# Feed-forward block on one core: the spill of the token features split by halves, and a token tile's feature chain begun one step earlier

## Chip, core and metric

The kernel runs on one core of a Trainium2 chip. The metric is the device time of one execution in microseconds (us). The timed runs gave a median of 756.93 us (756.38 to 761.38, 3 runs).

## What is computed

The reference is one transformer block on 4 x 1024 tokens of 512 channels (cut to what matters):

```
x = x + layernorm(attn(layernorm(x)))                 # attention over channels
h = layernorm(x)
gate, up = h @ gate_w.T, h @ up_w.T                   # 512 -> 2048
x = x + layernorm((silu(gate) * up) @ down_w.T)       # 2048 -> 512
```

The three feed-forward weights are not given as matrices: each is a cubic interpolation (Catmull-Rom) of a short list of control points. The change lies in the second half of the program, the feed-forward block.

## The kernel before

The first half (up to about 389 us) does the attention and prepares the interpolation. The feed-forward half works on 8 groups of 512 tokens. Because the weights are smooth, a token's normalised row is first reduced to *features* (moments of pieces of the row), and gate and up are products of these features with unit coefficients (`s_all`), which stay in SBUF.

**Groups, quads, steps.** A group has 16 steps, one for each 128 of the 2048 hidden units; four steps are a *quad* (`quad`, with j for the quad and s for the step in it), and a quad handles one token tile of 128 tokens of a later group as well. In step i the engines do, each in its own written order:

- TensorE (PE): the gate and up matmuls of two steps ahead into `gbank` and `ubank` (line 1542), every second step a moment matmul into `mbank` (line 1558), and a quarter of an output tile of the group before (`part`: lines 1572 to 1574 and 1583 to 1585, into `ybank`). In step 1 of a quad it transposes a token tile (`feats.turn`, line 1073, into `turned`), in step 2 it multiplies it with the feature table (`feats.products`, lines 1083 to 1088, into `zbank` and `turned`).
- ScalarE (ACT): SiLU of gate (line 1373, `gated`), the upper half of the product in 16 bits (line 1369), the scaling of an output tile (`o_norm`, line 1391), and for the features `h_hi` (line 1021, step 0) and `z_hi` (line 1031, step 3, twice).
- VectorE (DVE): the product of gate and up (line 1442, `inter`), the statistics of an output tile (`o_stats`, line 1462, step 1), its last step (`o_finish`, line 1473, `x_res`, step 2), and for the features the statistics (`feats.stats`, line 1039, step 1), the normalisation (`feats.norm`, line 1046, `xn`, step 3), `h_lo` (line 1051, step 0), the copy of the transposed tile out of PSUM (`turn_copy`, line 1056, `hT`, step 2) and `z_lo` (line 1062, step 3).
- GpSimd (POOL): the lower half of the product, a subtraction (line 1328), and in step 1 three small operations for an output tile (`o_scale`, lines 1335 to 1339) and two for the features (`feats.scale`, lines 1013 and 1015).

All engines wait on each other by semaphores that count. `gbank`, `ubank`, `zbank` and `turned` are single banks: the next matmul into one waits until the last reader is done. The gate matmul of step i+2 waits for SiLU of step i+1, the up matmul for the product of step i+1.

**From features to `z`.** The features of a group's four tiles are collected in `z_hi` and `z_lo`. When the fourth is done, in quad 1 of the group before, SP writes them to DRAM (`feats.spill`) and reads them back in another arrangement as `z`, the moving operand of gate and up (`ffn_in.load_z`). Each goes by halves: half 0 is what the first eight steps of a group need, half 1 the last eight. A spill of a half is three transfers, a load four, 256 KB each. `regroup` (line 1281) holds the order:

```
for half in range(2):
    sp.wait_ge(z_loaded[1 - par][half], loads_before * 64)
    feats.spill(sp, half, g, 1 - par)
for half in range(2):
    ffn_in.load_z(sp, feats, g, par, half)
```

`load_z` waits until the three spills of its half have landed. PE waits for half 0 at step 14 of the group before (its matmuls run two steps ahead), for half 1 at step 6 of the group itself. SP also stores the output tiles (`finish`, line 1271) and reloads `x_res` when a store has landed (`reload`, line 1267), and loads the tiles `x_ln` (line 987) for the features, all in one written order.

`made` and `begun` say whether a quad still has a feature tile to finish and one to begin: all quads of groups 0 to 5, in group 6 two and one, in group 7 none.

## Time and profile before

| what | value |
|---|---|
| median of 3 timed runs | 756.93 us |
| profiled execution: time, span | 758.16 us, 756.4 us |
| busy PE, DVE, POOL, ACT | 676.6, 512.7, 430.7, 365.5 us |
| mean granted TensorE clock | 0.955 of full |
| mean DMA rate | 152 GB/s |
| the chain that ended last: largest line | POOL act L1328, 8% of the span |

How to read it: the span is the time from the first to the last instruction of the profiled execution, and the time of that execution lies 1.76 us above its span. PE is the engine with the most work, but a share of busy time is a mean over two halves with different limits; what holds the feed-forward half is read from the waits inside it. The features feed PE through DVE, ACT, POOL and the DMA queue, so an engine that is not the busiest can still hold it.

### The profile page before, as it was taken

To read this page: it belongs to the slowest core of one execution; us is meant where nothing else is said; L and a number is where in the kernel's file an instruction comes from. 1 tells how busy PE (TensorE), PEld (TensorE's weight loads), DVE (VectorE), ACT (ScalarE), POOL (GpSimd) and SP (SyncE) were. 2 spreads that over 40 slices of the span, in tenths; PEclk is the share of its full clock that TensorE was granted. 3 is DMA by queue.
4 is the path that set the end of the run, shared out by engine and by line. 5 is a ranking of instruction groups with operands and counts; after the bars stand their busy time and mean duration, and the time that the engine had idled before them with its cause. 6 is when DMAs were issued, how large, how long until landed. Compare 5 with 4: busy or idle time off the path is not lost. (4 is left out here: it accounts for less than half of the span.)

```text
span 756.4 us, 16316 instructions
## 1 busy us (share of the span) xinstructions
PE 676.6 (89%) x5872; PEld 476.1 (63%) x5872; DVE 512.7 (68%) x993; ACT 365.5 (48%) x635; POOL 430.7 (57%) x615
## 2 busy tenths in 40 slices
PE   5996799999999999989947699898989899898996
PEld 3685686878687887867723255565655566564565
DVE  7666773588646973575656668887878878774653
ACT  3532232333232432333335677776777677574641
POOL 5269858547681958910425556564656546554642
PEclk9899899999999999999967899999999999998999
DMA  6814547324561447411786827567394946548123
GB/s 228 309 56 156 182 169 249 119 77 144 190 217 59 159 159 250 138 53 25 209 219 188 186 66 178 131 178 172 123 191 134 206 120 183 123 120 183 63 71 98
DMA packets 65549, 114.98 MB, mean 152 GB/s; under 512 B 12624, under 2 KB 29136, under 8 KB 65488
## 3 DMA queue, kind: packets, MB, share of 16 engines
q1 hardware_dynamic: 65488, 114.16, 52.4%
q8 instruction: 39, 0.64, 0.3%
q14 instruction: 22, 0.18, 0.1%
HBM read 81.76 MB, written 32.37 MB: 151 GB/s over the span
## 5 line engine op out<-in xcount | busy, mean ns | idle before, releaser
L1328 POOL TENSOR_TENSOR act<-inter,act 128x512 f16<-128x512 f32 x128 | 149.6, 1169 | 135.1 <-ACT act L1369 135.0
L1373 ACT ACTIVATE gated<-gbank,c_gate 128x512 f32<-128x512 f32 x128 | 88.0, 687 | 104.0 <-PE gbank L1542 104.0
L1442 DVE SCALAR_TENSOR_TENSOR inter<-ubank,c_up,gated 128x512 f32<-128x512 f32 x128 | 95.6, 747 | 49.8 <-ACT gated L1373 47.8
L1583 PE MATMUL ybank<-down,act 128*128 128x160 f16 x512 | 112.2, 238 | 0.0
L1584 PE MATMUL ybank<-down,act 128*128 128x160 f16 x512 | 111.5, 237 | 0.0
L1585 PE MATMUL ybank<-down,act 128*128 128x160 f16 x512 | 111.4, 236 | 0.0
L1369 ACT CAST act<-inter 128x512 f16<-128x512 f32 x128 | 78.2, 611 | 1.7 <-DVE inter L1442 1.7
L1583 PEld LDWEIGHTS ybank<-down,act 128*128 128x128 f16 x512 | 50.7, 99 | 39.2 <-issue 35.4
L1542 PE MATMUL gbank<-z,s_all 128*32 128x512 f16 x512 | 53.3, 407 | 24.3 <-DMA z<-token_features 15.9
L1542 PE MATMUL ubank<-z,s_all 128*32 128x512 f16 x512 | 52.7, 402 | 8.3 <-DVE inter L1442 7.5
L1584 PEld LDWEIGHTS ybank<-down,act 128*128 128x128 f16 x512 | 51.0, 100 | 3.8
L1585 PEld LDWEIGHTS ybank<-down,act 128*128 128x128 f16 x512 | 51.1, 100 | 0.0
L633 DVE SCALAR_TENSOR_TENSOR tu_lo<-chain,tu_hi 128x512 fp32r<-128x512 f32 x32 | 22.1, 690 | 42.6 <-ACT tu_hi L501 42.5
L1473 DVE SCALAR_TENSOR_TENSOR x_res<-y,orr,x_res 128x512 f32<-128x512 f32 x32 | 41.0, 1282 | 13.1 <-ACT y L1391 13.1
L369 POOL TENSOR_TENSOR yr<-ymv,eps 128x1 f32<-128x1 f32 x32 | 19.9, 621 | 50.4 <-DVE ymv L717 50.3
L501 ACT ACTIVATE tu_hi<-chain 128x512 fp32r<-128x512 f32 x32 | 19.1, 597 | 57.8 <-PE chain L792 57.8
L1542 PEld LDWEIGHTS gbank<-z,s_all 128*32 128x32 f16 x512 | 13.2, 93 | 52.7 <-DMA z<-token_features 17.1
L790 PE MATMUL chain<-z_hi 128*128 128x512 f16 (+3 forms) x128 | 37.9, 307 | 7.7 <-DVE z_lo L618 7.7
L501 ACT ACTIVATE ga_hi<-chain 128x512 fp32r<-128x512 f32 (+3 forms) x32 | 16.5, 518 | 53.3 <-PE chain L792 53.3
L1558 PE MATMUL mbank<-act,basis 128*32 128x512 f16 x512 | 41.4, 402 | 0.6 <-POOL act L1328 0.6
L411 POOL TENSOR_TENSOR job<-job 128x640 f32<-128x640 f32 x24 | 38.2, 1593 | 1.7 <-DMA job<-job_in 1.7
L791 PE MATMUL chain<-z_lo,z_hi 128*128 128x512 f16 (+3 forms) x128 | 38.2, 307 | 0.0
(195 smaller groups left out, 1943.5 us busy)
## 6 DMA issues: line engine op xcount, KB each, us to landing
x_ln<-x SPq DMA_DIRECT2D x64, 256.0 KB, 3.5
z<-token_features SPq DMA_DIRECT2D x64, 256.0 KB, 5.9
job<-job_in SPq DMA_DIRECT2D x24, 640.0 KB, 4.3
shared<-x SPq DMA_DIRECT2D x32, 256.0 KB, 2.7
x<-shared SPq DMA_DIRECT2D x32, 256.0 KB, 2.0
token_features<-z_hi SPq DMA_DIRECT2D x32, 256.0 KB, 4.2
x_res<-x SPq DMA_DIRECT2D x32, 256.0 KB, 2.7
out<-x_res SPq DMA_DIRECT2D x32, 256.0 KB, 2.1
```

The lines of the kernel that those rows point to most:

```text
L411: pool.tensor_tensor(job[:, k % 2, 0], job[:, k % 2, 0], job[:, k % 2, 1], ALU.mult).then_inc(job_mult, 1)
L791: pe.matmul(out, l_hi, r_lo, start=False, stop=False)
L1328: pool.tensor_tensor(hidden[par][:, i, TOK:2 * TOK], inter[:, i % INTERS, :], hidden[par][:, i, 0:TOK], ALU.subtract).then_inc(inter_ready, 1)
L1369: act.copy(hidden[par][:, i, 0:TOK], inter[:, i % INTERS, :]).then_inc(inter_hi_done, 1)
L1373: act.activation(gated[:, slot % 2, :], gbank[:], ACT.Silu, scale=c_gate[:]).then_inc(silu_done, 1)
L1442: dve.scalar_tensor_tensor(out=inter[:, i % INTERS, :], in0=ubank[:], scalar=c_up[:], in1=gated[:, i % 2, :], op0=ALU.mult, op1=ALU.mult). ...
L1473: dve.scalar_tensor_tensor(out=x_res[:, q % 2, :], in0=y[:, q % 2, :], scalar=orr[:, q, 2:3], in1=x_res[:, q % 2, :], op0=ALU.subtract, op ...
L1542: mm = pe.matmul(bank[rows], s_all[:, side, c, w, rows], z[par][:, i // 4 * 4 + u, :], start=True, stop=True)
L1558: mm = pe.matmul(bank[32 * col:32 * col + 32], basis[:, r, 32 * half:32 * half + 32], hidden[par][:, r, part * TOK:(part + 1) * TOK], star ...
L1583: pe.matmul(out, hidden[par][:, r, high], box[:, 0], start=False, stop=False)
L1584: pe.matmul(out, hidden[par][:, r, high], box[:, 1], start=False, stop=False)
L1585: mm = pe.matmul(out, hidden[par][:, r, low], box[:, 0], start=False, stop=False)
```

## The change

Two parts, with no instruction added to a quad and none taken away.

- **Halves.** `regroup` takes one half at a time: spill half 0 and load half 0 at the end of quad 1, spill half 1 and load half 1 at the end of quad 2.
- **Feature chain.** Of the tile that a quad begins, the statistics move from step 1 to step 0, `norm` from step 3 to step 2, and `h_hi` and `h_lo` from step 0 of the next quad to step 3 of this one. Of the tile that it finishes, the transposes on PE move from step 1 to step 0 and `turn_copy` from step 2 (ahead of the product) to step 1 (behind the product, ahead of the output statistics); `products`, `z_hi` and `z_lo` stay. `h_hi` and `h_lo` of one tile are made ahead of the first quad.

```diff
--- before.py
+++ after.py
@@ -1278,14 +1278,12 @@
                 else:
                     load_res(g + 1, q - 2)
 
-            def regroup(g, par, loads_before):
-
-
-                for half in range(2):
-                    sp.wait_ge(z_loaded[1 - par][half], loads_before * 64)
-                    feats.spill(sp, half, g, 1 - par)
-                for half in range(2):
-                    ffn_in.load_z(sp, feats, g, par, half)
+            def regroup(g, par, half, loads_before):
+
+
+                sp.wait_ge(z_loaded[1 - par][half], loads_before * 64)
+                feats.spill(sp, half, g, 1 - par)
+                ffn_in.load_z(sp, feats, g, par, half)
 
             def quad(g, par, count, j, made, begun, more):
                 for ahead in ((0,), (1, 2, 3), (), ())[j] if more else ():
@@ -1296,8 +1294,8 @@
                     for before, q in outputs(g, i, 2):
                         finish(before, q)
                         reload(before, q)
-                if j == 1 and not (isinstance(g, int) and g == GROUPS - 1):
-                    regroup(g + 1, 1 - par, count)
+                if j in (1, 2) and not (isinstance(g, int) and g == GROUPS - 1):
+                    regroup(g + 1, 1 - par, j - 1, count)
 
             feats.load(sp, x1_t, Q + 3, 3)
             ffn_in.load_z(sp, feats, 0, 0, 1)
@@ -1411,8 +1409,8 @@
                         moment_hi(g - 1, 1)
                     if i == I - 1:
                         moment_hi(g, 0)
-                    if s == 0 and made:
-                        feats.high(act, g * Q + j + AHEAD)
+                    if s == 3 and begun:
+                        feats.high(act, g * Q + j + AHEAD + 1)
                     if s == 3 and made:
                         feats.z_high(act, g * Q + j + AHEAD, (j + 2) % Q, g + 1, z_banks, par if j < 2 else 1 - par)
 
@@ -1421,6 +1419,7 @@
             feats.high(act, Q + 1)
             high(0, 0, 0, 0)
             feats.z_high(act, Q + 1, 1, 1, z_banks)
+            feats.high(act, Q + 2)
             schedule(act, quad)
             moment_hi(GROUPS - 1, 1)
             o_norm(GROUPS - 2, Q - 1)
@@ -1479,10 +1478,10 @@
                 for s in range(4):
                     i = 4 * j + s
                     n = g * I + i
-                    if s == 2 and made:
-                        feats.turn_copy(dve, m, z_banks)
                     if not (isinstance(n, int) and n >= STEPS - 2):
                         product(n + 2, i + 2)
+                    if s == 1 and made:
+                        feats.turn_copy(dve, m, z_banks)
                     if i == 0 and not (isinstance(g, int) and g == 0):
                         moment_lo(g - 1, 1)
                     if i == I - 1:
@@ -1494,14 +1493,14 @@
                         o_stats(before, q)
                     for before, q in outputs(g, i, 2):
                         o_finish(before, q)
-                    if s == 0 and made:
-                        feats.low(dve, m)
-                    if s == 1 and begun:
+                    if s == 0 and begun:
                         feats.stats(dve, m + 1, (j + AHEAD + 1) % RING, loads)
+                    if s == 2 and begun:
+                        feats.norm(dve, m + 1, (j + 1 + AHEAD) % RING)
                     if s == 3 and made:
                         feats.z_low(dve, m, (j + 2) % Q, z_banks, par if j < 2 else 1 - par)
                     if s == 3 and begun:
-                        feats.norm(dve, m + 1, (j + 1 + AHEAD) % RING)
+                        feats.low(dve, m + 1)
 
             feats.stats(dve, Q + 1, 1, 2)
             feats.norm(dve, Q + 1, 1)
@@ -1512,6 +1511,7 @@
             feats.stats(dve, Q + 2, 2, 2)
             feats.z_low(dve, Q + 1, 1, z_banks)
             feats.norm(dve, Q + 2, 2)
+            feats.low(dve, Q + 2)
             schedule(dve, quad)
             moment_lo(GROUPS - 1, 1)
             y_out(GROUPS - 2, Q - 1)
@@ -1612,7 +1612,7 @@
                         moment_pair(g, i // 2 - 1, par)
                     if not first:
                         part(g - 1, i, 1 - par)
-                    if s == 1 and made:
+                    if s == 0 and made:
                         feats.turn(pe, m, z_banks, id16)
                     if s == 2 and made:
                         feats.products(pe, m, z_banks)
```

On DVE, in a quad of the loop that also finishes an output tile, there stood before (from the output statistics of step 1 to the normalisation in step 3; `inter` is the product, `ostats` and `omv` the output statistics, `hstats` and `hmv` those of the features):

```order
L1462 BN_STATS ostats<-y 128x6
L1464 MEMSET carrier 128x1
L1465 BN_AGGR omv<-ostats 128x2
L1039 BN_STATS hstats<-x_ln 128x6
L1041 MEMSET hcarrier 128x1
L1042 BN_AGGR hmv<-hstats 128x2
L1056 COPY hT<-turned 128x1024
L1442 SCALAR_TENSOR_TENSOR inter<-ubank,c_up,gated 128x512
L1473 SCALAR_TENSOR_TENSOR x_res<-y,orr,x_res 128x512
L1442 SCALAR_TENSOR_TENSOR inter<-ubank,c_up,gated 128x512
L1062 SCALAR_TENSOR_TENSOR z_lo<-zbank,z_hi 128x4x128
L1046 TENSOR_SCALAR xn<-x_ln,hmv,hr 128x512
```

And now (from the product of step 1 to the product of the next quad's step 0; the lines of this block are numbered one lower here):

```order
L1441 SCALAR_TENSOR_TENSOR inter<-ubank,c_up,gated 128x512
L1056 COPY hT<-turned 128x1024
L1461 BN_STATS ostats<-y 128x6
L1463 MEMSET carrier 128x1
L1464 BN_AGGR omv<-ostats 128x2
L1441 SCALAR_TENSOR_TENSOR inter<-ubank,c_up,gated 128x512
L1472 SCALAR_TENSOR_TENSOR x_res<-y,orr,x_res 128x512
L1046 TENSOR_SCALAR xn<-x_ln,hmv,hr 128x512
L1441 SCALAR_TENSOR_TENSOR inter<-ubank,c_up,gated 128x512
L1062 SCALAR_TENSOR_TENSOR z_lo<-zbank,z_hi 128x4x128
L1051 SCALAR_TENSOR_TENSOR h_lo<-xn,h_hi 128x512
L1441 SCALAR_TENSOR_TENSOR inter<-ubank,c_up,gated 128x512
```

The copy of `hT` has moved from behind both statistics to ahead of the output statistics; the feature statistics have left this stretch; `xn` (norm) stands between `x_res` (o_finish) and the product of step 3; `h_lo` stands ahead of the next product in place of behind it.

On SP, in the group change, there stood before (three spills per half, then eight loads, then a store of an output tile and a reload):

```order
L998 DMA token_features<-z_hi 64x2048
L999 DMA token_features<-z_hi 64x2048
L1002 DMA token_features<-z_lo 64x2048
L998 DMA token_features<-z_hi 64x2048
L999 DMA token_features<-z_hi 64x2048
L1002 DMA token_features<-z_lo 64x2048
L1146 DMA z<-token_features 32x8x512 x8
L1271 DMA out<-x_res 128x512
L1267 DMA x_res<-x 128x512
```

And now:

```order
L998 DMA token_features<-z_hi 64x2048
L999 DMA token_features<-z_hi 64x2048
L1002 DMA token_features<-z_lo 64x2048
L1146 DMA z<-token_features 32x8x512 x4
L1271 DMA out<-x_res 128x512
L1267 DMA x_res<-x 128x512
L998 DMA token_features<-z_hi 64x2048
L999 DMA token_features<-z_hi 64x2048
L1002 DMA token_features<-z_lo 64x2048
L1146 DMA z<-token_features 32x8x512 x4
```

The four loads of half 0 stand right behind half 0's spills, and a store and a reload stand between them and half 1's spills.

## Rows read from the trace of the kernel before

**Rows 1.** Waits from 385 us on: engine, line, releaser: us in total, times, longest.

```profile
PE gbank L1542 <- DMA z<-token_features: 15.9, 7, 3.5
```

**Rows 2.** Timeline of PE around a group change: start us, us, engine, line, operation, tiles.

```profile
516.32 0.40 PE L1542 MATMUL gbank<-z,s_all 128*32 128x512 f16 x4 [2.35 <-DMA z<-token_features]
```

**Rows 3.** Timeline of SP's DMA queue, 500 to 550 us, the same columns.

```profile
501.54 0.47 SPq L998 DMA_DIRECT2D token_features<-z_hi  x1
...
503.40 1.67 SPq L998 DMA_DIRECT2D token_features<-z_hi  x1
...
507.40 5.70 SPq L1146 DMA_DIRECT2D z<-token_features  x8
```

**Rows 4.** Stretches: length, busy PE, PEld, DVE, ACT, POOL, clock, DMA share, GB/s.

```profile
517.00:521.00 4.00, 4.00 (x44) 3.34 (x36) 1.78 (x2) 1.59 (x3) 1.16 (x1) 0.57 0.98 204
...
689.10:695.00 5.90, 5.86 (x48) 3.40 (x49) 2.53 (x3) 3.46 (x6) 1.53 (x2) 0.52 0.82 165
```

**Rows 5.** Timeline of PE in an undisturbed quad, 533 to 544 us.

```profile
533.79 0.39 PE L1542 MATMUL ubank<-z,s_all 128*32 128x512 f16 x4
...
537.51 0.39 PE L1073 MATMUL turned<-ident,h_hi 128*128 128x128 f16 x4
...
538.05 0.40 PE L1542 MATMUL gbank<-z,s_all 128*32 128x512 f16 x4
...
543.69 0.39 PE L1542 MATMUL ubank<-z,s_all 128*32 128x512 f16 x4
```

**Rows 6.** Timeline of DVE, then ACT, then POOL in the same quad.

```profile
534.70 0.54 DVE L1046 TENSOR_SCALAR xn<-x_ln,hmv,hr 128x512 f32<-128x512 f32 x1
...
537.30 0.75 DVE L1442 SCALAR_TENSOR_TENSOR inter<-ubank,c_up,gated 128x512 f32<-128x512 f32 x1 [0.26 <-ACT gated L1373]
537.96 0.68 DVE L1462 BATCH_NORM_STATS2 ostats<-y 128x6 f32<-128x512 f32 x1
...
539.62 0.66 DVE L1056 COPY hT<-turned 128x1024 f16<-128x1024 f16 x1
540.19 0.74 DVE L1442 SCALAR_TENSOR_TENSOR inter<-ubank,c_up,gated 128x512 f32<-128x512 f32 x1
...
539.82 0.72 ACT L1391 ACTIVATE y<-y,orr 128x512 f32<-128x512 f32 x1
...
540.78 1.16 POOL L1328 TENSOR_TENSOR act<-inter,act 128x512 f16<-128x512 f32 x1
```

**Rows 7.** Timeline of DVE, PE and ACT in quads without features, 676 to 757 us.

```profile
676.58 0.75 DVE L1442 SCALAR_TENSOR_TENSOR inter<-ubank,c_up,gated 128x512 f32<-128x512 f32 x1 [1.16 <-ACT gated L1373]
...
677.25 0.68 DVE L1462 BATCH_NORM_STATS2 ostats<-y 128x6 f32<-128x512 f32 x1
...
677.39 0.40 PE L1542 MATMUL ubank<-z,s_all 128*32 128x512 f16 x4
...
679.10 0.72 ACT L1391 ACTIVATE y<-y,orr 128x512 f32<-128x512 f32 x1 [0.56 <-POOL orr L1337]
...
679.96 1.04 DVE L1473 SCALAR_TENSOR_TENSOR x_res<-y,orr,x_res 128x512 f32<-128x512 f32 x1 [1.13 <-ACT y L1391]
...
741.57 0.75 DVE L1473 SCALAR_TENSOR_TENSOR x_res<-y,orr,x_res 128x512 f32<-128x512 f32 x1
```

**Rows 8.** Timeline of DVE beside POOL, in the attention and at 526.8 us.

```profile
69.91 1.48 DVE L613 TENSOR_SCALAR xn<-x_ln,mv,rstd 128x512 f32<-128x512 f32 x1 [4.80 <-POOL rstd L363]
71.31 1.21 DVE L618 SCALAR_TENSOR_TENSOR z_lo<-xn,z_hi 128x512 f16<-128x512 f32 x1
...
69.84 1.26 POOL L389 TENSOR_TENSOR units<-units 128x512 f32<-128x512 f32 x1
71.18 0.79 POOL L391 TENSOR_TENSOR units<-units 128x256 f32<-128x256 f32 x1
...
526.85 0.68 DVE L1051 SCALAR_TENSOR_TENSOR h_lo<-xn,h_hi 128x512 f16<-128x512 f32 x1
...
527.13 1.41 POOL L1328 TENSOR_TENSOR act<-inter,act 128x512 f16<-128x512 f32 x1 [0.96 <-ACT act L1369]
```

## Prediction

> **What bounds the kernel now.** I read the busy shares first, then the waits of TensorE in the feed-forward half (from 389 us on), then the order of SP's transfers around one such wait, then one undisturbed quad on all engines. TensorE (PE) is the busiest engine, and in the feed-forward half it sets the pace: its steps follow each other with small gaps, except at one place in each group. There the first gate matmul of the next group finds its features not yet loaded. That is seven waits, 15.9 us in all [rows 1]. In group 2 the matmul that starts at 516.32 had been waiting for 2.35 us, so it was wanted at 513.97 [rows 2]. SP's list shows why: the first spill of half 0 is issued at 501.54, the first spill of half 1 at 503.40, and the eight loads go out only from 507.40, behind all six spills [rows 3]. All 14 transfers of 256 KB each (32 x 8 x 512 values of 2 bytes in a load) share the 16 DMA engines, and half 0's loads, the only ones that are wanted soon, land last but four.
>
> After four of the seven waits the granted clock falls to 1.2 GHz: it is 0.57 of full in the 4 us behind the wait at 516.32 and 0.52 in the 5.9 us behind the last one [rows 4]; the stretches behind the waits at 602 and 646 read like the first.
>
> Without such a wait a quad (four steps) takes 9.90 us, from one ubank matmul of step 0 to the next (533.79 to 543.69) [rows 5].
>
> **The change part by part.** *Spill and load by halves.* It removes the three spills of half 1 and nothing else from in front of half 0's four loads; SP's rows keep their number. Half 0's loads may go once its own spills have landed. SP had issued these by 503.40 and the loads at 507.40 [rows 3], so the start can move forward by 0 to 2 us; I take 1, to 506.4. Then four loads, 1.05 MB, stand alone in the queues. At the 204 GB/s of a stretch full of these transfers [rows 4] that is 5.1 us; with half 1's bytes in front of and among them they took 8.9 (507.40 to 516.32 [rows 2, 3]). So half 0 is there between 511.5 and 515.3, and is wanted at 513.97; I take the lower half of this, since nothing else is queued. The seven waits go: -15.9 us (bounds -15.9 and 0). Half 1 is now sent a quad later and is wanted eight steps (two quads) after half 0, which leaves it more room than it has now. SP is behind the new wait with out and x_res of the output tiles; before, the same two stood behind eight loads.
>
> The half-clock stretches behind the waits go with them. They hold back 4.0 x 0.43 = 1.7 us (three such stretches) and 5.9 x 0.48 = 2.8 us, 8.0 us in all [rows 4]; some of this is spent waiting for other engines anyway. I take -7 (bounds -8 and 0).
>
> By the Trainium skill (DMA: Bandwidth & Descriptors, section Anatomy of one DMA, fitted there to transfers that GpSimd issues) a transfer costs about 2 us plus its bytes at 436 GB/s, which would put half 0 in SBUF some 4.4 us after its loads' issue, an estimate, early enough in any case. The trace does not agree on the rate: 204 GB/s with the engines 98% busy [rows 4]. By that rule rival E below could be struck out; by the row it keeps a small chance.
>
> *The feature chain spread over the steps.* Per quad no instruction is added on any engine. On PE the eight transposes move from step 1 to step 0, on VectorE (DVE) turn_copy goes from step 2 to step 1 and stands now ahead of the output statistics, norm from step 3 to step 2, h_lo from the next step 0 to step 3; ScalarE (ACT) makes h_hi ahead of z_hi in step 3. PE's work per quad stays, so the question is whether anything is late. I follow DVE from its product of step 1 round to the same product of the next quad, each term from a row.
> Product of step 1 to the next DVE instruction: 0.66 (537.30 to 537.96). turn_copy, new here: 0.57 (539.62 to 540.19) [rows 6]. Start of the output statistics to the scaling on ACT, through three small POOL operations: 1.85 (677.25 to 679.10). From there to the start of o_finish on DVE: 0.86 (to 679.96). o_finish by itself: 0.75 (741.57) [rows 7].
> Now comes norm, whose scale POOL makes just ahead of its own subtraction (line 1328). These two can't run side by side. At 69.91 a normalisation of the same form and size was stretched to 1.48 and ended at 71.39, 0.29 behind POOL's addition (to 71.10). POOL's next operation was issued at 71.18 and DVE's next at 71.31, and that one took 1.21, that is, POOL went first though DVE had just had the turn. The other way round, POOL's subtraction that was issued at 527.13 into DVE's h_lo (to 527.53) took 1.41 in place of 1.16 and ended 1.01 behind it [rows 8]. So: o_finish, then POOL's subtraction +1.01, then norm +0.29, and the next DVE instruction 0.08 before that ends.
> That instruction is the product of step 3. Product to the ubank matmul that it frees: 0.81 (676.58 to 677.39) [rows 7]. From ubank of step 0 through the rest of that step, the gate of step 1 and its activation to the product of step 1: 3.51 (533.79 to 537.30) [rows 5, 6], plus the transposes that stand in step 0 now, 0.54 (537.51 to 538.05) [rows 5].
> Sum: 0.66 + 0.57 + 1.85 + 0.86 + 0.75 + 1.01 + 0.29 - 0.08 + 0.81 + 3.51 + 0.54 = 10.77 us. PE's own work, 9.90 at most, is shorter: the quad is now set by this ring, +0.87. Before, norm was not in the ring, and turn_copy stood behind the statistics. It holds for the 20 quads of groups 1 to 5 and the first of group 6, where all parts are there: 21 x 0.87 = +18.3 us. Bounds: per quad +0.03 (rival B) and +1.93 (rival C). In group 0 there are no outputs and hence no o_finish, but norm meets POOL's subtraction too: 0 to 4 x 0.87, and the extra h_hi and h_lo ahead of the first quad stand before step 0; +2 for both, an estimate from the same term (bounds 0 and +4).
>
> By the Trainium skill (SBUF — State Buffer, section SBUF: two separate sides) VectorE and GpSimd share a pair of ports as an exclusive lock, held for a whole instruction by the one that starts first; an instruction with two SBUF inputs or in a two-port mode needs it. The rule speaks against bringing norm beside POOL's subtraction; by it alone rival B falls out, and the trace agrees in the pairs of rows 8. It does not say which of two waiting engines comes next; only the pair at 71.18 and 71.31 does.
>
> Sum of all: -15.9 - 7 + 18.3 + 2 = -2.6 us. The profiled execution took 758.16 us (span 756.4), so 755.6; it lies 1.2 above the median of the three runs, so on their scale 754.4 to 755.6. I say 755.
>
> **The rivals.** *B, norm keeps the port behind o_finish.* Then the 1.01 + 0.29 - 0.08 in the ring become 0.38 (a norm of 0.54 as at 534.70 [rows 6], with 0.08 overlapped at either end), 0.84 less: a quad of 9.93, almost as today, and what counts is the removed waits: 755 - 21 x 0.84 = 737. For it: DVE's instruction is at hand the moment o_finish ends. Against it: the pair at 71.18 and 71.31 [rows 8].
> *C, POOL's subtraction gets in ahead of o_finish (slower).* From o_norm on ACT (539.82) to the subtraction on POOL (540.78) it is 0.96, to o_finish 0.86 [rows 6, 7]: a margin of 0.10. If it is lost, o_finish ends 0.55 behind the subtraction (0.96 + 1.16 + 0.55 = 2.67 after o_norm), the subtraction of step 3 is by then waiting and takes +1.01, norm +0.29 - 0.08: 3.89 in place of 2.83, +1.06 in each of 21 quads: 755 + 22 = 777. It decides from a tenth of a microsecond on.
> *D, the clock.* In the forecast PE idles for about a microsecond in each quad, in two pieces. A fall of the clock once a group, at the 1.7 us of rows 4, six times, would add 10: 765. Against it: PE's short waits of today leave the clock at full speed in undisturbed quads.
> *E, half 0 lands no earlier.* If the landing of its spills sets the start and not half 1's bytes, the waits stay, 23 us come back: 778. For it: how soon half 0's spills land when nothing follows them no row shows.
>
> **How the numbers follow.** Forecast 0.45, B (with what lies between it and the forecast) 0.24, C 0.14, D 0.12, E 0.05. A measurement of this kernel tells about 1% from no change, here 7.6 us. Faster by more: B and a tail of the forecast, 0.28. Slower by more: C, E, half of D and a tail, 0.27. Within: 0.45. The forecast's own range is 747 to 763 (the ring's sum is uncertain by 0.2 us a quad, 4 in all, the clock and group 0 by 4 more). For 8 in 10 the range must reach close to B and C: 738 to 777.
>
> **What would show it.** Right: no wait of PE for the z loads; o_finish at 0.75, with POOL's subtraction, issued just behind it, stretched to about 1.7; norm at about 1.4 in place of 0.54; quads of 10.8 us; waits of ubank for DVE's product at step 0 of each quad. Wrong: norm at 0.54 and quads of 9.9 (B); o_finish still at 1.04 or more and quads near 11.8 (C); gate still waiting for z loads once a group (E); a granted clock under full speed in most groups (D).

## The result and the profile after

| | before | after |
|---|---|---|
| median | 759.15 us (756.38 to 763.58, 4 runs) | 767.66 us (765.32 to 770.81, 4 runs) |
| profiled execution: time, span | 758.16 us, 756.4 us | 770.81 us, 769.0 us |
| mean granted clock | 0.955 | 0.948 |

The changed kernel takes 1.0137 times as long, with a 95% interval from 1.0091 to 1.0183: slower, where 755 us and no measurable change were forecast. The profiled execution of the changed kernel is the slowest of its four, so its trace shows a little more loss (12.6 us of span) than the medians do (8.5 us).

The gate matmuls of step 0 are good marks for an account. In the timeline of PE of the kernel before, the first gates issued in group 0, group 1, group 6 and the last gate of all:

```profile
398.63 0.62 PE L1542 MATMUL gbank<-z,s_all 128*32 128x512 f16 x4
436.97 0.40 PE L1542 MATMUL gbank<-z,s_all 128*32 128x512 f16 x4 [0.58 <-ACT gated L1373]
652.70 0.40 PE L1542 MATMUL gbank<-z,s_all 128*32 128x512 f16 x4
724.26 0.40 PE L1542 MATMUL gbank<-z,s_all 128*32 128x512 f16 x4
```

And the same four of the changed kernel:

```profile
400.30 0.62 PE L1542 MATMUL gbank<-z,s_all 128*32 128x512 f16 x4
444.50 0.40 PE L1542 MATMUL gbank<-z,s_all 128*32 128x512 f16 x4 [0.58 <-ACT gated L1371]
664.96 0.40 PE L1542 MATMUL gbank<-z,s_all 128*32 128x512 f16 x4
736.88 0.40 PE L1542 MATMUL gbank<-z,s_all 128*32 128x512 f16 x4
```

From row to row: 1.7 us are lost ahead of group 0, 5.9 in group 0 (38.3 to 44.2), 4.7 in groups 1 to 5 (215.7 to 220.5), 0.4 in groups 6 and 7, and nothing behind the last gate: 12.6 us. The first 1.7 can't be told from chance, though the extra `h_hi` and `h_lo` stand there: in the profiles of all the runs below that mark lies at 397.3 to 400.3 with them and at 398.6 to 401.5 without.

The waits of PE from 385 us on (us in total, times, longest) answer to [rows 1]:

```profile
PE ubank L1542 <- DVE inter L1441: 28.2, 38, 2.7
PE turned L1073 <- DVE h_lo L1051: 7.3, 5, 2.3
PE gbank L1542 <- DMA z<-token_features: 2.8, 1, 2.8
```

Of the seven waits for features one is left, at the end of group 6. In their place PE waits 38 times for DVE's product, and in group 0 its transposes wait for `h_lo`, up to 2.3 us. Before, the waits for the product were

```profile
PE ubank L1542 <- DVE inter L1442: 7.5, 9, 2.7
```

and no transpose of group 0 waited longer than 0.63.

One quad of group 3 (j = 0) in the changed kernel, from the timelines of DVE, ACT, POOL and PE, answers to [rows 5 to 7]:

```profile
540.16 0.75 DVE L1441 SCALAR_TENSOR_TENSOR inter<-ubank,c_up,gated 128x512 f32<-128x512 f32 x1
541.87 0.75 DVE L1472 SCALAR_TENSOR_TENSOR x_res<-y,orr,x_res 128x512 f32<-128x512 f32 x1 [0.95 <-ACT y L1389]
542.53 1.38 DVE L1046 TENSOR_SCALAR xn<-x_ln,hmv,hr 128x512 f32<-128x512 f32 x1
543.84 0.74 DVE L1441 SCALAR_TENSOR_TENSOR inter<-ubank,c_up,gated 128x512 f32<-128x512 f32 x1
...
541.01 0.72 ACT L1389 ACTIVATE y<-y,orr 128x512 f32<-128x512 f32 x1 [1.70 <-POOL orr L1335]
...
541.99 2.94 POOL L1326 TENSOR_TENSOR act<-inter,act 128x512 f16<-128x512 f32 x2
...
538.72 0.40 PE L1542 MATMUL ubank<-z,s_all 128*32 128x512 f16 x4 [1.08 <-DVE inter L1441]
...
544.63 0.40 PE L1542 MATMUL ubank<-z,s_all 128*32 128x512 f16 x4 [0.80 <-DVE inter L1441]
```

It is the picture that the prediction drew: o_finish at 0.75, POOL's subtraction at hand 0.12 us behind it and next in turn, norm stretched to 1.38 (it was 0.54 at 534.70 in [rows 6]), the product behind norm, and the ubank matmul of the next quad's step 0 waiting for that product. The two subtractions in the POOL row take 2.94 together, 2.3 when undisturbed.

SP's list at a group change, answering to [rows 3], and in group 6 with the gate that waits:

```profile
511.99 0.47 SPq L998 DMA_DIRECT2D token_features<-z_hi  x1
...
517.47 3.05 SPq L1146 DMA_DIRECT2D z<-token_features  x4
...
695.38 1.80 SPq L1146 DMA_DIRECT2D z<-token_features  x4
...
702.89 0.62 PE L1542 MATMUL gbank<-z,s_all 128*32 128x512 f16 x4 [2.77 <-DMA z<-token_features]
```

From half 0's first spill to its loads it takes 5.5 us here, where it took 5.9 in [rows 3]; but over all seven group changes it is 5.5 to 6.0, and it was 5.6 to 5.9, with a mean of 5.7 in both kernels. From the loads to the gate that waits for them it takes 7.5, where [rows 2, 3] have 8.9.

Group 0 as a whole and the 5 us behind that last wait, in windows of the changed kernel (stretch, us, busy PE, PEld, DVE, ACT, POOL, granted clock, DMA share, GB/s):

```profile
400.30:444.50 44.20, 32.41 (x282) 13.56 (x281) 27.61 (x45) 24.12 (x44) 20.09 (x23) 0.59 0.58 150
703.00:708.00 5.00, 5.00 (x50) 2.90 (x47) 2.37 (x3) 3.13 (x6) 1.20 (x2) 0.70 0.63 175
```

And group 0 of the kernel before:

```profile
398.63:436.97 38.34, 26.53 (x282) 11.87 (x282) 24.46 (x44) 24.02 (x44) 20.30 (x23) 0.79 0.73 181
```

Group 0 runs at a mean clock of 0.59 in place of 0.79, with the same matmuls. PE stands idle for 11.8 us in both windows; the 5.9 us are all in its busy time, at the lower clock. One of its four quads shows a wait that the kernel before has not at this length:

```profile
424.61 0.69 DVE L1062 SCALAR_TENSOR_TENSOR z_lo<-zbank,z_hi 128x512 f16<-128x512 f32 x1 [1.26 <-ACT z_hi L1031]
425.22 0.68 DVE L1051 SCALAR_TENSOR_TENSOR h_lo<-xn,h_hi 128x512 f16<-128x512 f32 x1
...
425.96 0.23 PE L1073 MATMUL turned<-ident,h_hi 128*128 128x128 f16 x1 [1.72 <-DVE h_lo L1051]
```

The transposes of step 0 need `h_lo`, which DVE makes behind `z_lo` of the step before. In later groups the output matmuls of the step stand ahead of the transposes and cover this; in group 0 there are none.

### The profile page after: what moved, and what is told of

It reads as the page before. It is cut to its first block and busy times, and to the rows that moved or that the text cites. A ratio compares the mean times of both kernels' runs of the same rounds, so it can differ in the third digit from the quotient of the medians.

```text
span 769.0 us, 16316 instructions
## 1 busy us (share of the span) xinstructions
PE 682.0 (89%) x5872; PEld 474.6 (62%) x5872; DVE 518.8 (67%) x993; ACT 367.8 (48%) x635; POOL 443.6 (58%) x615
## 5 line engine op out<-in xcount | busy, mean ns | idle before, releaser
L1326 POOL TENSOR_TENSOR act<-inter,act 128x512 f16<-128x512 f32 x128 | 161.4, 1267 | 120.0 <-ACT act L1367 120.0
L1583 PE MATMUL ybank<-down,act 128*128 128x160 f16 x512 | 110.4, 235 | 0.0
L1584 PE MATMUL ybank<-down,act 128*128 128x160 f16 x512 | 109.5, 233 | 0.0
L1585 PE MATMUL ybank<-down,act 128*128 128x160 f16 x512 | 109.5, 233 | 0.0
L1583 PEld LDWEIGHTS ybank<-down,act 128*128 128x128 f16 x512 | 50.1, 98 | 37.5 <-issue 33.7
L1584 PEld LDWEIGHTS ybank<-down,act 128*128 128x128 f16 x512 | 50.3, 98 | 3.8
L1585 PEld LDWEIGHTS ybank<-down,act 128*128 128x128 f16 x512 | 50.3, 98 | 0.0
L1472 DVE SCALAR_TENSOR_TENSOR x_res<-y,orr,x_res 128x512 f32<-128x512 f32 x32 | 26.1, 815 | 31.8 <-ACT y L1389 31.8
L1542 PEld LDWEIGHTS ubank<-z,s_all 128*32 128x32 f16 x512 | 13.4, 95 | 49.3 <-DVE inter L1441 49.0
L1389 ACT ACTIVATE y<-y,orr 128x512 f32<-128x512 f32 x32 | 23.1, 721 | 42.9 <-POOL orr L1335 42.9
L1046 DVE TENSOR_SCALAR xn<-x_ln,hmv,hr 128x512 f32<-128x512 f32 x32 | 39.5, 1234 | 4.6 <-POOL hr L1015 4.6
```

Source lines behind the costliest of these rows:

```text
L1046: dve.tensor_scalar(self.xn[:, 0, :], self.x_ln[:, slot, :], self.hmv[:, 0:1], self.hr[:, 1:2], ALU.subtract, ALU.mult).then_inc(self.h_no ...
L1326: pool.tensor_tensor(hidden[par][:, i, TOK:2 * TOK], inter[:, i % INTERS, :], hidden[par][:, i, 0:TOK], ALU.subtract).then_inc(inter_ready, 1)
L1389: act.activation(y[:, q % 2, :], y[:, q % 2, :], ACT.Copy, scale=orr[:, q, 1:2]).then_inc(o_normed, 1)
L1542: mm = pe.matmul(bank[rows], s_all[:, side, c, w, rows], z[par][:, i // 4 * 4 + u, :], start=True, stop=True)
L1583: pe.matmul(out, hidden[par][:, r, high], box[:, 0], start=False, stop=False)
L1584: pe.matmul(out, hidden[par][:, r, high], box[:, 1], start=False, stop=False)
```

## Experiments

Eleven kernels, each compared with the kernel before on the same chip (its medians beside them: 760.08, 758.39, 759.53 and 758.57 us). A quad's length is from its first gate matmul to that of the next quad. "..." marks lines left out.

**The two parts apart.** First the kernel before with the halves alone (and `regroup` taking one half at a time, as in the change):

```
-                if j == 1 and not (isinstance(g, int) and g == GROUPS - 1):
-                    regroup(g + 1, 1 - par, count)
+                if j in (1, 2) and not (isinstance(g, int) and g == GROUPS - 1):
+                    regroup(g + 1, 1 - par, j - 1, count)
```

> The kernel before with only the spill and load by halves. Theory (from the changed kernel's trace: half 0's loads go out 5.5 us behind its first spill in place of 5.9, and the four alone take 7.5 us to land in place of 8.9): half 0 lands 1.3 us sooner, so of the waits of 2.1 to 2.4 us in groups 1 to 5 about 1 us each stays, quads of 9.9 stay, and the time falls by 5 to 12 us, to 747 to 754. Rival (the step on record): the seven waits go and the half clock behind them too, 23 us less, 734 to 740. Second rival: nothing lands sooner and the time stays at 757 to 760.

Measured: 742.79 us beside 760.08, ratio 0.9779 (0.9705 to 0.9852). The waits for features, and the longest of them with SP's rows ahead of it:

```profile
PE gbank L1540 <- DMA z<-token_features: 6.7, 5, 3.4
...
661.63 0.34 SPq L1267 DMA_DIRECT2D x_res<-x  x1
662.08 0.45 SPq L998 DMA_DIRECT2D token_features<-z_hi  x1
...
668.56 1.80 SPq L1146 DMA_DIRECT2D z<-token_features  x4
...
676.61 0.40 PE L1540 MATMUL gbank<-z,s_all 128*32 128x512 f16 x4 [3.39 <-DMA z<-token_features]
```

Two waits are gone, four are down to 0.6 to 1.2 us, and the last stays at 3.4. So the waits shrink as the theory said; the time lies between the theory's 747 and the rival's 740, because the clock stays at 1.00 in the 4 us behind each of the four short waits: the quads with a short wait take 10.1 to 10.7 us, where before three took 13.4.

Then the feature chain alone, the changed kernel with the old group change (and the old `regroup`):

```
-                if j in (1, 2) and not (isinstance(g, int) and g == GROUPS - 1):
-                    regroup(g + 1, 1 - par, j - 1, count)
+                if j == 1 and not (isinstance(g, int) and g == GROUPS - 1):
+                    regroup(g + 1, 1 - par, count)
```

> The changed kernel with the old group change (both halves spilled, then both loaded); the feature chain stays as changed. Theory: the longer quads (group of 44.4 us) give half 0 16.7 us from the end of quad 1, and by the old order it lands 16.8 us behind it, so the waits stay under 0.3 us a group; only the one at the end of group 6 grows from 2.8 to about 3.5 or 4. Time 766 to 771, like the changed kernel. Rival (the halves are what removed the waits): waits of 2 us and half clock in each group again, 16 to 23 us more than the changed kernel, 783 to 790.

Measured: 772.45 us beside 760.08, ratio 1.0170 (1.0118 to 1.0222), with

```profile
PE gbank L1544 <- DMA z<-token_features: 7.7, 5, 4.1
```

of which one is 4.05 and the others 0.7 to 1.4. A little over what the theory gave, far from the rival's 783. So the halves are worth 17.3 us in the kernel before and only 4 to 5 beside the new chain (+12.4 without them, +8.5 with them; 772.45 and 767.66 by the medians): the longer quads alone give half 0 most of the time that it lacked. The parts don't add: -17.3 and +12.4 would make -4.9, and it was +8.5.

**The ring.** POOL's subtraction of step 2 taken out of norm's way, in the changed kernel:

```
-                    if not (isinstance(n, int) and n == STEPS - 1):
+                    if s != 2 and not (isinstance(n, int) and n == STEPS - 1):
                         low(n + 1, (i + 1) % I, par if i + 1 < I else 1 - par)
+                    if s == 1:
+                        low(n + 2, i + 2, par)
```

> The changed kernel, with POOL's subtraction of step 2 issued in step 1, ahead of the output tile's three small operations, so that it no longer runs into o_finish and norm; no other engine's order changes. Theory (the port lock makes the ring): norm falls from 1.37 to 0.55 us, the product of step 3 comes about 0.9 us sooner, undisturbed quads take 9.9 in place of 10.8, 21 x 0.9 = 19 us less, of which waits for half 0 (1 us a group) may take 5 back: 748 to 755. Rival (the copy of hT ahead of the output statistics and the transposes in step 0 make the quad longer, not the lock): quads of 10.5 or more, 763 to 770. Second rival: the subtraction delays the small operations, o_norm and o_finish by as much as it saves; norm at 0.55 and quads still at 10.5 or more.

Measured: 768.57 us beside 760.08, ratio 1.0109 (1.0045 to 1.0173). The second rival held in the main:

```profile
544.77 1.16 POOL L1326 TENSOR_TENSOR act<-inter,act 128x512 f16<-128x512 f32 x1 [0.32 <-ACT act L1369]
545.88 0.19 POOL L1333 TENSOR_TENSOR orr<-omv,heps 128x1 f32<-128x1 f32 x1
...
547.59 0.75 DVE L1474 SCALAR_TENSOR_TENSOR x_res<-y,orr,x_res 128x512 f32<-128x512 f32 x1 [1.92 <-ACT y L1391]
548.25 0.54 DVE L1046 TENSOR_SCALAR xn<-x_ln,hmv,hr 128x512 f32<-128x512 f32 x1
```

Norm is back at 0.54 with nothing else changed on DVE, so the subtraction is what stretched it. But the output tile's small operations now wait for the same subtraction, DVE's wait for o_norm grows from 0.95 to 1.92, and most of the saving goes: the quads of group 2 take 11.88, 10.32, 11.18 and 10.42, 0.6 us less in all than in the changed kernel. The time as a whole hides two more things. Group 0, which has no output tiles, falls from 44.2 to 41.7 us, and group 7, which has no features, grows by 4.3, its quads from 8.65 to 9.83, since the subtraction moved there too. So the time by itself doesn't tell whether the ring sets the quad; the quads of the next two do.

The copy of `hT` behind the output statistics:

```
-                    if s == 1 and made:
-                        feats.turn_copy(dve, m, z_banks)
...
                     for before, q in outputs(g, i, 1):
                         o_stats(before, q)
+                    if s == 1 and made:
+                        feats.turn_copy(dve, m, z_banks)
```

> The changed kernel, with the copy of hT behind the output statistics of step 1 in place of ahead of them; nothing else moves. Theory (the ring of the prediction sets the quad, and this copy is 0.57 us of it): the undisturbed quad falls from 10.8 to 10.2 us, 21 x 0.57 = 12 less, 754 to 758 beside 767.7 of the changed kernel. Rival (the ring is closed elsewhere, by the transposes in step 0 or by norm alone): quads stay at 10.7 or more and the time at 764 to 769. Second rival: the products in step 2 now wait for the copy and give half of it back, 760 to 764.

Measured: 755.18 us beside 758.39, ratio 0.9968 (0.9945 to 0.9991). The quads of group 2 went from 11.72, 10.83, 11.13 and 10.74 to 11.14, 10.23, 10.54 and 10.14: 0.58 to 0.60 each, for a term of 0.57. So this copy is a link of what sets the quad, at its full price, as the prediction had it.

Norm ahead of o_finish, in the time in which DVE waits for o_norm, and its scale on POOL ahead of the output tile's:

```
+                    if s == 1 and begun:
+                        feats.scale(pool, g * Q + j + AHEAD + 1)
                     for before, q in outputs(g, i, 1):
                         o_scale(before, q)
...
+                    if s == 2 and begun:
+                        feats.norm(dve, m + 1, (j + 1 + AHEAD) % RING)
                     for before, q in outputs(g, i, 2):
                         o_finish(before, q)
```

> The changed kernel, with norm ahead of o_finish on DVE, in the microsecond in which DVE waits there, and the feature scale ahead of the output tile's on POOL, so that norm can run then. Theory (port lock, and whoever comes first goes first): norm takes 0.55 us and costs the ring nothing; POOL's subtraction of step 2 is at hand when its small operations end, about 0.4 us ahead of o_norm's end, so it gets in ahead of o_finish, which waits for it and takes about 1.3 to 1.8 by the profile; product of step 3 about 0.7 us sooner than in the changed kernel, quads of 10.0 to 10.2, time 752 to 757. Rival (norm or its clash doesn't decide): quads of 10.7 or more, 764 to 770. Second rival: norm holds up the small operations, o_norm and o_finish come as much later: 762 to 768 with norm at 0.55.

Measured: 753.97 us beside 758.39, ratio 0.9941 (0.9912 to 0.9970).

```profile
542.48 0.54 DVE L1046 TENSOR_SCALAR xn<-x_ln,hmv,hr 128x512 f32<-128x512 f32 x1
543.94 1.04 DVE L1472 SCALAR_TENSOR_TENSOR x_res<-y,orr,x_res 128x512 f32<-128x512 f32 x1 [0.92 <-ACT y L1389]
...
543.28 1.16 POOL L1326 TENSOR_TENSOR act<-inter,act 128x512 f16<-128x512 f32 x1
```

As expected, norm costs 0.54, and the subtraction, issued 0.66 ahead of o_finish, goes first; o_finish ends 0.54 behind it, the 0.55 that rival C was priced with. The quads fall to 9.85 and 10.25 (j = 1 and 2), and with them the short waits for half 0 come back (7.1 us in six, by the waits). The clash with POOL's subtraction, not norm's own 0.54, was the price.

**Group 0.** The transposes of group 0 alone back in step 1:

```
-                    if s == 0 and made:
+                    if s == (1 if first else 0) and made:
                         feats.turn(pe, m, z_banks, id16)
```

> The changed kernel, with the eight transposes of group 0 (and only there) back in step 1 on PE. Theory: in group 0 there are no output matmuls ahead of the transposes, so in step 0 PE waits for h_lo (1.1 to 2.4 us in each of four quads) and stays at half clock; behind step 1's matmuls these waits fall under 0.7 us, group 0 takes 38 to 41 us in place of 44.2, and the time falls by 3 to 6 us, to 761 to 765. Rival (norm's clash with POOL's subtraction in group 0, as the record had it, makes the group long): group 0 stays at 43 us or more and the time at 767 to 769.

Measured: 765.98 us beside 760.08, ratio 1.0092 (1.0063 to 1.0121), and the window of group 0:

```profile
397.33:438.13 40.80, 28.76 (x283) 13.13 (x282) 26.91 (x45) 24.45 (x44) 20.22 (x23) 0.72 0.58 156
```

Group 0 falls by 3.4 us, as the theory said; the time by only 1.7, less than expected and inside the scatter of the runs (by 2.6 when each is taken beside the kernel before on its chip: +5.9, where it was +8.5). To this the statistics, also back in step 1 in group 0:

```
+                    if s == 1 and begun and isinstance(g, int) and g == 0:
+                        feats.stats(dve, m + 1, (j + AHEAD + 1) % RING, loads)
                     if s == 1 and made:
                         feats.turn_copy(dve, m, z_banks)
...
-                    if s == 0 and begun:
+                    if s == 0 and begun and not (isinstance(g, int) and g == 0):
                         feats.stats(dve, m + 1, (j + AHEAD + 1) % RING, loads)
```

> The changed kernel, with two edits undone in group 0 alone: the transposes back in step 1 on PE (as in an earlier run, where group 0 fell from 44.2 to 40.8 us) and the feature statistics back in step 1 on DVE. Theory (what made group 0 long are these two; the statistics alone, put into step 0 in another kernel, had cost it 3.6 us): group 0 at 36.5 to 38.5 us, the time 760 to 763. Rival (norm in front of step 3's product and its clash with POOL's subtraction, as the record had it, is what is left): group 0 at 40 to 41 us, the time at 765 to 767.

Measured: 764.70 us beside 758.57, ratio 1.0080 (1.0047 to 1.0112); group 0 takes 39.5 us (397.95 to 437.42). Neither held: the statistics give 1.3 back, not the 2.3 to 4.3 of the theory. The 38.3 of the kernel before hold a wait for features of 1.1 us, which the change removes; the halves alone take 36.7 in group 0 (400.22 to 436.91), and against that 2.8 are left. Norm is still stretched here, to 1.15 to 1.32 in group 0, where it took 0.54 before. What that costs the run with POOL's subtraction out of its way had shown, with norm at 0.55 in group 0:

```profile
397.91:439.65 41.74, 27.34 (x281) 12.71 (x280) 24.32 (x45) 24.10 (x44) 20.23 (x23) 0.76 0.57 154
```

That is 2.5 less than 44.2. The three prices, 3.4, 1.3 and 2.5, make 7.2 of the 7.5 between 44.2 and 36.7, if they add; no run undid all three.

**Towards a faster kernel.** In the run with the halves alone SP reloads `x_res` ahead of the spills, and that waits for a store to land. So, on the kernel before, the halves with this order:

```
...
+                for before, q in stored:
+                    finish(before, q)
+                if regroup:
+                    spill_half(g + 1, 1 - par, j - 1, count)
+                for before, q in stored:
+                    reload(before, q)
+                if regroup:
+                    ffn_in.load_z(sp, feats, g + 1, 1 - par, j - 1)
```

Here `stored` are the output tiles of the quad, and `spill_half` is `regroup` without the loads.

> The kernel before with the halves, and in quads 1 and 2 the spills issued ahead of the reload of x_res, which waits for a store to land; the loads behind it. Theory (half 0 lands too late by SP's order: its first spill went out 1.5 us and its last 2 us after the features were ready): half 0 lands 1.2 to 2 us sooner, the waits of 0.6 to 1.2 us in groups 2 to 5 go, the one at the end of group 6 falls from 3.4 to 1.5 to 2, with half its half-clock stretch: 3 to 6 us less than the halves alone (742.8), 736 to 740. Rival (the landing of the spills, not their issue, sets it, and the store of the output tile that lands later shares the queues): no change, 742 to 744.

Measured: 736.85 us beside 758.39, ratio 0.9732 (0.9691 to 0.9774).

```profile
657.48 0.45 SPq L998 DMA_DIRECT2D token_features<-z_hi  x1
...
659.28 1.21 SPq L1267 DMA_DIRECT2D x_res<-x  x1
662.97 1.93 SPq L1146 DMA_DIRECT2D z<-token_features  x4
...
669.96 0.40 PE L1541 MATMUL gbank<-z,s_all 128*32 128x512 f16 x4 [0.29 <-DMA z<-token_features]
```

Group 6's third quad starts at 660.45 with the halves alone and at 656.90 here. Behind that start the first spill goes out after 0.6 us in place of 1.6 and the loads after 6.1 in place of 8.1, and of all waits for features one of 0.29 us is left.

To this the statistics of the feature tile, one step sooner as the change has them:

```
-                    if s == 1 and begun:
+                    if s == 0 and begun:
                         feats.stats(dve, m + 1, (j + AHEAD + 1) % RING, loads)
```

> The same, and of the feature chain only the statistics one step sooner (step 0, behind h_lo), as the change has them; norm, h_hi, h_lo, transposes and the copy stay where they were. Theory (the statistics stand ahead of the copy of hT in step 1 and make the products wait 0.26 to 0.36 us for it in 16 quads, and o_finish meets POOL's subtraction through the late feature scale): the waits for hT go, 3 to 6 us less than with the spills first alone, 732 to 737. Rival: the statistics in step 0 delay the product of step 1 by as much, no change or up to 5 us more, 737 to 745.

Measured: 744.72 us beside 758.39, ratio 0.9828 (0.9790 to 0.9866): 7.9 more than without this move. The waits for `hT` of about 0.3 us are gone, but

```profile
PE ubank L1541 <- DVE inter L1441: 17.1, 32, 2.7
```

PE now waits 32 times for a product, 9 times (7.7 us) with the spills first alone. Group 0 went from 36.6 to 40.2 us and the quads with j = 0 from 10.72 to 11.06. (Of the 8.7 us between the two spans 2.9 lie ahead of group 0, where the profiles differ by chance, 3.6 in group 0 and 1.9 in groups 1 to 5.)

And the other way, the statistics one step later, in step 2 behind the product, and the feature scale on POOL a step later as well:

```
-                    if s == 1 and begun:
+                    if s == 2 and begun:
                         feats.scale(pool, g * Q + j + AHEAD + 1)
...
+                    if s == 2 and begun:
+                        feats.stats(dve, m + 1, (j + AHEAD + 1) % RING, loads)
                     for before, q in outputs(g, i, 2):
                         o_finish(before, q)
...
-                    if s == 1 and begun:
-                        feats.stats(dve, m + 1, (j + AHEAD + 1) % RING, loads)
```

> The kernel before with the halves and the spills first, and the feature statistics a step later (step 2, behind the product, in the time in which DVE waits for o_norm) in place of sooner; the feature scale on POOL a step later as well. Theory (the copy of hT is late because the feature statistics stand ahead of it): the copy comes 0.7 us sooner, the waits for it of 0.26 to 0.36 us in 22 quads go, 4 to 7 us less than 736.9: 730 to 733. Rival (the feature scale behind POOL's subtraction makes norm late, or the statistics delay o_finish): no gain or up to 5 us more, 737 to 742.

Measured: **728.07 us** (725.58 to 729.39) beside 759.53, ratio 0.9569 (0.9539 to 0.9598), the fastest of all.

```profile
538.80 0.66 DVE L1056 COPY hT<-turned 128x1024 f16<-128x1024 f16 x1
539.37 0.74 DVE L1441 SCALAR_TENSOR_TENSOR inter<-ubank,c_up,gated 128x512 f32<-128x512 f32 x1
540.03 0.68 DVE L1039 BATCH_NORM_STATS2 hstats<-x_ln 128x6 f32<-128x512 f32 x1
...
540.86 0.86 DVE L1472 SCALAR_TENSOR_TENSOR x_res<-y,orr,x_res 128x512 f32<-128x512 f32 x1
...
540.01 1.16 POOL L1327 TENSOR_TENSOR act<-inter,act 128x512 f16<-128x512 f32 x1
```

The copy stands behind one set of statistics in place of two, the waits for it of about 0.3 us are gone, and quads take 9.42 in place of 9.88. That is 8.8 us less than the spills first alone, where the theory had 4 to 7. The other 0.15 of a quad was not taken apart; the row of o_finish shows one thing more: it takes 0.86, with the spills first alone 1.65 to 1.69, since the statistics now fill part of the time in which POOL's subtraction held it up.

Last, the changed kernel with four of the edits above together: the copy behind the statistics, norm ahead of o_finish, group 0's transposes in step 1, the spills first. The feature statistics stay in step 0.

> The changed kernel with all that the runs so far point to: the copy of hT behind the output statistics, norm ahead of o_finish, the transposes of group 0 in step 1, and the spills ahead of the reload. Theory (the ring was the chain's only fault in groups 1 to 6): the ring is shorter than PE's own work, the waits for hT stay away, quads of 9.4 to 9.7 in place of 9.9, against 4 us more in group 0 than the kernel before: 728 to 737, at or under the 736.9 of the spills first without any chain. Rival (o_finish still behind POOL's subtraction, and the transposes in step 0 in front of the next gate): quads of 9.9 or more, 738 to 746, so that the earlier chain is worth nothing even then.

Measured: 745.12 us beside 759.53, ratio 0.9785 (0.9750 to 0.9819). The rival's time held: quads of 11.21, 9.71, 10.13 and 9.91 in group 2, and 41 us in group 0. So with these edits the earlier chain is still slower than the spills first without it (736.85). Why was not tested: the 8.3 us between them are close to the 7.9 that the early statistics cost by themselves, and a chain without these was not run.

## Why the prediction was wrong, point by point

**The seven waits and the half clock behind them: -22.9 forecast, -16.1 measured.** Before, the last quads of groups 1 to 5 took 11.70, 13.44, 11.59, 13.42 and 13.38, 14.2 us more than five of 9.86, and that went entirely. (The step had 16.4 for these five: 15.9 less the 1.1 of group 0, which is counted with group 0 below, and the 3.5 of the last, and three stretches of 1.7 [rows 1, 4]; some of that time passed in other waits.) The last quad of group 6 went only from 14.54 to 12.65, where 8.74 was to be had (the spills first).

Here a step failed: "I take 1" for the sooner start and the lower half of 511.5 to 515.3 for the landing. The loads went out no sooner (5.7 us behind the first spill in the mean of either kernel), so the landing of half 0's own spills sets their start, as rival E, at 0.05, had it. And they landed 7.5 us behind their issue, not 5.1; with the halves alone it was 7.3 to 8.1. From 507.40 that makes 514.9, 0.9 later than the 513.97 at which half 0 is wanted, and waits of 0.6 to 1.2 us are what the halves alone left. E's price, all 23 us, did not come about, since 7.5 is still less than 8.9. The first spill, too, went out late, behind the reload of `x_res`, which the prediction had passed over: the run with the spills first took 5.9 us less than the halves alone. By the Trainium skill (DMA: Bandwidth & Descriptors, section Anatomy of one DMA, fitted there to transfers that GpSimd issues) the four loads would have taken an estimated 4.4 us; the trace has 7.5, and the measurement decides. And what removed the waits in groups 1 to 5 need not have been the halves: the longer quads alone nearly do it.

**The ring: +18.3 forecast, +21.2 measured.** The mechanism was right, and so was the sum: 10.77 a quad, against 10.83 and 10.74 for j = 1 and 3. It was too small for the quads j = 0 (11.72, before 10.7) and above all j = 2 (11.13, before 9.86), which makes 1.9 of the 2.9. Here a term was put at nothing: the prediction took 9.90 for every quad and gave the statistics in step 0 no price. In these two quads they stand behind the copy of an output tile (at j = 0 behind `mom_lo` as well), the product of step 1 comes late, and PE waits for it once more: 1.08 at j = 0 (538.72), and at j = 2

```profile
560.67 0.40 PE L1542 MATMUL ubank<-z,s_all 128*32 128x512 f16 x4 [0.48 <-DVE inter L1441]
```

No run moved the statistics alone out of the changed kernel; moved in alone, with the spills first, they lengthened the same two quads, by 0.34 and 0.10. In groups 1 to 5 the ring's share is 4.7 + 14.2 = 18.9, and 2.2 in group 6, which without the rounding is 21.2.

**Group 0: +2 forecast, bounds 0 and +4; measured +5.9, outside them.** This step failed. The clash of norm with POOL's subtraction that it priced is there, with norm at 1.37 in all four quads, and is worth 2.5 by the run that took the subtraction away. What it put at nothing are PE's transposes, moved to a step in which group 0 has nothing to cover them, 3.4 us by the first experiment on it, and the statistics, 1.3. All of the 5.9 is busy time of PE, at a clock of 0.59 in place of 0.79.

**The sum.** The three terms missed by 6.8, 2.9 and 3.9 us, all to the slow side, and the start of the feed-forward half came 1.7 later by chance: 15.3, against 15.2 from the sum of -2.6 to the 12.6 of the spans. Any one of the misses would have turned the small gain of the sum into a loss, and no one of them mended would have turned the measured loss into a gain; the first, the feature wait of group 6 and its clock above all, is the largest. That 767.7 lies between 738 and 777 is luck: the upper end was set by C and E, and neither came about at its price.

**The rivals.** B fell: POOL went ahead of norm in all 20 full quads. C had its margin at 0.12 us (0.10 was worked out) and never came about in a full quad of the changed kernel; putting norm first made it happen, at the price given. In the kernel before it was there already, in the quad of [rows 6], behind the subtraction of 540.78:

```profile
540.85 1.64 DVE L1473 SCALAR_TENSOR_TENSOR x_res<-y,orr,x_res 128x512 f32<-128x512 f32 x1
```

D fell: the granted clock is 1.00 in windows from 445 to 695 us. By the Trainium skill (SBUF — State Buffer, section SBUF: two separate sides) VectorE and GpSimd hold the pair of ports that they share one at a time; the rows of norm at 1.38 and 0.54 agree.

## What to carry to other kernels

Price an instruction that is moved at every place where it lands, in the groups that lack the usual cover too (here group 0), and also one that seems free on an engine with idle time (here the statistics). Two parts that relieve the same wait don't add: run each alone before a change is kept or dropped, for here one half of a losing change was worth 2.2%. And before a chain is begun sooner, see what stands in front of its critical link; moving the statistics later won what moving them sooner lost.

## What the runs showed of the hardware beyond what was expected

The feature statistics (0.68 us, one input of 128 x 512 in 32 bits) ran at full speed beside POOL's subtraction (540.03 to 540.71 beside 540.01 to 541.17 in the fastest kernel, both at their usual length), where norm, with an input of the same size, was stretched to 1.38 by it. What an instruction on DVE costs beside POOL therefore depends on which instruction it is. With the halves alone, the granted clock was 1.00 behind the wait of 1.23 us (513 to 519 us) and 0.72 behind the one of 3.39 (676 to 682).
